# Masked row maxima in attention: the diagonal mask moves from a matrix product into the maximum instruction

## The reference

```
attn = einsum('bhqd,bhkd->bhqk', q, k) / sqrt(hd)
attn = attn + alibi
attn = where(causal, attn, finfo.min)
p    = softmax(attn, axis=-1)
out  = einsum('bhqk,bhkd->bqhd', p, v).reshape(Bb, Tt, C) @ Wo + bo
```

## Time and profile before

| | us |
|---|---|
| median of 3 runs | 1429.78 (1424.3 to 1432.53) |
| span of the profiled execution | 1444.0 |
| main part of the attention stage in it (395 to 960 from the start of the span) | 565 |

### The profile page before, as it was taken

One profiled execution on the slowest core, in us unless ns is written; L12 is line 12 of the kernel. 1 busy time (PEld: TensorE's weight loads), 2 busy tenths in 40 slices (PEclk: granted clock), 3 DMA queues, 4 the chain that ended last, 5 costly groups with the idle time before them and its releaser, 6 DMA issues. The chain is left out here.

```text
span 1444.0 us, 20692 instructions
## 1 busy us (share of the span) xinstructions
PE 1081.1 (75%) x6895; PEld 632.7 (44%) x6896; DVE 790.8 (55%) x2091; ACT 517.8 (36%) x814; POOL 501.2 (35%) x538
## 2 busy tenths in 40 slices
PE   5762149903898999999999989887476877676676
PEld 4651136702244444444454444433244766565443
DVE  4757810044867787878778887761252333333326
ACT  1330013403066556655566545554211221111113
POOL 3110064055016101520154103342444256665633
PEclk9975568955589999999999989987699898999898
DMA  4226013323213111311222121013431432222135
GB/s 117 73 63 109 1 39 106 92 43 91 67 28 97 36 37 47 97 36 36 73 80 80 44 68 52 25 38 143 164 102 34 105 86 77 82 80 63 37 107 185
DMA packets 90021, 106.09 MB, mean 73 GB/s; under 512 B 16882, under 2 KB 69883, under 8 KB 87285
## 3 DMA queue, kind: packets, MB, share of 16 engines
q1 hardware_dynamic: 76862, 79.08, 19.1%
q0 software_dynamic: 13072, 25.90, 6.5%
HBM read 63.29 MB, written 37.95 MB: 70 GB/s over the span
## 5 line engine op out<-in xcount | busy, mean ns | idle before, releaser
L2005 DVE TENSOR_REDUCE maxima<-psum 128x1 f32<-128x512 f32 (+4 forms) x624 | 390.7, 644 | 118.7 <-PE psum L1825 60.7
L1939 ACT ACTIVATE probs<-psum 128x1024 f32<-128x1024 f32 (+3 forms) x384 | 300.6, 809 | 306.8 <-PE psum L1840 237.5
L1820 PE MATMUL psum<-ka,qa 75*128 75x512 bf16 (+3 forms) x768 | 245.4, 352 | 42.6 <-DVE maxima L2005 30.3
L1836 PE MATMUL psum<-qa,ka 78*128 78x512 bf16 (+3 forms) x768 | 211.0, 337 | 4.3 <-ACT probs L1939 4.0
L116 POOL DMA_INDIRECT expert_out<-g_y,g_place x160 | 155.2, 970 | 123.2 <-issue 88.1
L1853 PE MATMUL psum<-probs,v_wide 128*32 128x512 f32 (+3 forms) x1536 | 171.5, 520 | 0.0
L1820 PEld LDWEIGHTS psum<-ka,qa 75*128 75x128 bf16 x768 | 69.6, 101 | 188.7 <-DVE maxima L2005 143.6
L1357 POOL DMA_INDIRECT got<-expert_out,to_row x64 | 66.4, 1038 | 188.0 <-ACT probs L1939 128.4
L2475 DVE TENSOR_TENSOR g_y<-psum,g_gate 128x512 f32<-128x512 f32 x40 | 27.7, 692 | 154.4 <-DMA expert_out<-g_y,g_place 139.3
L1836 PEld LDWEIGHTS psum<-qa,ka 78*128 78x128 bf16 x768 | 75.5, 101 | 79.0 <-ACT probs L1939 28.7
L1840 PE MATMUL psum<-mask_k,ident_b 128*128 128x128 bf16 x512 | 107.1, 228 | 0.0
(11 more groups left out here) (325 smaller groups left out, 1653.2 us busy)
## 6 DMA issues: line engine op xcount, KB each, us to landing
g_rows<-sorted SPq DMA_DIRECT2D x160, 65.0 KB
qa<-q_steps SPq DMA_DIRECT2D x45, 192.0 KB
ka<-k_steps SPq DMA_DIRECT2D x15, 576.0 KB
f_got<-expert_out SPq DMA_DIRECT2D x16, 512.0 KB, 11.1
w<-in_W SPq DMA_DIRECT2D x16, 256.0 KB
w_gu<-in_gu SPq DMA_DIRECT2D x1, 4096.0 KB, 18.6
q_steps<-q_parts SPq DMA_DIRECT2D x12, 256.0 KB
k_steps<-k_parts SPq DMA_DIRECT2D x12, 256.0 KB
```

What stands on the lines that cost most here:

```text
L1820: mm = pe.matmul(bank[:, h * width:(h + 1) * width], qa[b][0:ROWS_MAX, h0 + h, qt * P:(qt + 1) * P], ka[b][0:ROWS_MAX, h0 + h, seg * HALF: ...
L1836: mm = pe.matmul(out, ka[s.buf][0:ROWS_ALL, h, j * P:(j + 1) * P], qa[s.buf][0:ROWS_ALL, h, q0:(c + 1) * HALF], start=True, stop=True, ski ...
L1939: act.activation(probs[k % PRING][:, 2 * pair:2 * pair + 2, 0:w], PS[:, 2 * pair:2 * pair + 2, 0:w], ACT.Exp).then_inc(exps, 1)
L2005: dve.tensor_reduce(maxima[:, seg, h0:h0 + heads, qt], bank[:, 0:heads * width].rearrange("p (h k) -> p h k", h=heads), AX.X, ALU.max).the ...
```

## The change

The 512 mask products of the maxima pass go. `mask_q` (bf16, 128 columns) becomes `mask_wide` (fp32, 512 columns: zeros, then the triangle in the last 128), and VectorE adds its last `width` columns in the same instruction that takes the maximum: `tensor_tensor_reduce`, once for each head instead of once for each unit. It writes the masked scores, which nobody reads, to `masked` (bf16, two buffers), and the maximum to `accum_out`. A wait on `small_read` guards the buffer of two units back. Units below the diagonal keep `tensor_reduce`; the main pass's mask stays a product.

```diff
-        ident_b, mask_q, mask_k = ...
+        ident_b, mask_k = M.sb("ident_b", [P, P], bf16), M.sb("mask_k", [P, P], bf16)
+        mask_wide, masked = M.sb("mask_wide", [P, HALF]), M.sb("masked", [P, 2, HALF], bf16)
...
-                pool.memset(mask_q[:], 0.0).then_inc(preset, 1)
+                pool.memset(mask_wide[:], 0.0).then_inc(preset, 1)
...
-                        if seg * HALF + width == (qt + 1) * P:
-                            for h in range(heads):
-                                mm = pe.matmul(bank[:, (h + 1) * width - P:(h + 1) * width], ident_b[:], mask_q[:],
-                                               start=False, stop=True, skip_group_check=True)
...
+                        if seg * HALF + width == (qt + 1) * P:
+                            if number >= 2:
+                                dve.wait_ge(small_read, number - 1)
+                            for h in range(heads):
+                                last = dve.tensor_tensor_reduce(
+                                    out=masked[:, number % 2, h * width:(h + 1) * width], in0=bank[:, h * width:(h + 1) * width],
+                                    in1=mask_wide[:, HALF - width:HALF], scale=1.0, scalar=LOWEST, op0=ALU.add, op1=ALU.max,
+                                    accum_out=maxima[:, seg, h0 + h, qt:qt + 1])
+                            last.then_inc(small_read, 1)
+                        else:
+                            dve.tensor_reduce(maxima[:, seg, h0:h0 + heads, qt],
+                                              bank[:, 0:heads * width].rearrange("p (h k) -> p h k", h=heads),
+                                              AX.X, ALU.max).then_inc(small_read, 1)
```

More of the change, by code:

```diff
@@ L52 @@
 ROWS_MAX, ROWS_ALL = PROD + 3, PROD + 6
-MASKED = -1.0e30
+MASKED, LOWEST = -1.0e30, -3.0e38
 SCORE_SCALE = float(1 / np.sqrt(np.float32(HD)))
@@ L1642, in stage_attention @@
         recips = [M.sb(f"recip{c}", [P, 4, GH, 2]) for c in range(2)]
-        ident_b, mask_q, mask_k = M.sb("ident_b", [P, P], bf16), M.sb("mask_q", [P, P], bf16), M.sb("mask_k", [P, P], bf16)
+        ident_b, mask_k = M.sb("ident_b", [P, P], bf16), M.sb("mask_k", [P, P], bf16)
+        mask_wide, masked = M.sb("mask_wide", [P, HALF]), M.sb("masked", [P, 2, HALF], bf16)
         max_here = [M.sem(f"max_rows_here{b}") for b in range(BUFS)]
@@ L1728, in _ @@
                                    base=0, pattern=[[-1, P]], channel_multiplier=1).then_inc(masks, 1)
-                pool.affine_select(out=mask_q[:], in_=mask_q[:], compare_op=ALU.is_ge, fill=MASKED,
+                pool.affine_select(out=mask_wide[:, HALF - P:HALF], in_=mask_wide[:, HALF - P:HALF], compare_op=ALU.is_ge, fill=MASKED,
                                    base=0, pattern=[[-1, P]], channel_multiplier=1).then_inc(masks, 1)
@@ L2004, in emit_small @@
                         qt, seg, h0, heads, width = u
-                        dve.tensor_reduce(maxima[:, seg, h0:h0 + heads, qt],
-                                          bank[:, 0:heads * width].rearrange("p (h k) -> p h k", h=heads),
-                                          AX.X, ALU.max).then_inc(small_read, 1)
+                        if seg * HALF + width == (qt + 1) * P:
[11 more added lines that the diff above has]
+                                              AX.X, ALU.max).then_inc(small_read, 1)
                         if u == MAX_UNITS[-2]:
```

## The result

The changed kernel takes 1454.8 us (median of 4 runs, 1444.4 to 1460.4), the kernel before 1427.8. The ratio is 1.018 (95% interval 1.013 to 1.022): slower by 1.8%, where 1419 us was forecast. A second set of runs of the same kernel gave 1.016 (1.007 to 1.025).

A forecast was written before the change was run, and what follows sets the result against it. TensorE was taken to set the pace in most of slots 0 to 9, VectorE in slots 10 and 11. The terms -12 + 2 - 3 + 2 + 0 gave -11 us: 1419 us median, range 1406 to 1465.

The forecast's parts named there:

- What bounds the kernel: Attention stage: TensorE sets the pace in most of slots 0 to 9; slots 10 and 11 wait for VectorE.
- The terms for them, -12 and +2 us: Slots 0 to 9: 12 us gained from removed mask products, 2 us lost to longer many-head units on VectorE.
- The price of the new instruction: VectorE: it takes the plain sum's 281, 418, 555 and 692 ns; the accumulator read costs nothing start to start.
- the half-rate rival: New instruction at half rate, VectorE setting the pace everywhere: 110 us more, 1540; chance 0.06.
- Slots 10 and 11 by hand: Units followed one by one in step 3: about 0.2 us gained, 14 times, 3 us.
- The added wait: VectorE's wait on small_read, 23 times a step: up to 3 us lost, taken as 2.
- the time ahead of step 0: 48 units at half clock ahead of step 0: gains and losses cancel, taken as 0.
- the sum: Whole kernel: -12 + 2 - 3 + 2 + 0 = -11 us, 1419 for the median.
- "a few us": Allowance for the clock in the lower end of the range, beside -16.5 and -3 us.
- a sign to look for afterwards: Sign of being wrong: granted clock of the stretch below 0.96 because TensorE idles more.
- The rival on the other side: VectorE becomes the pace, a head costing 0.15 us above the sum's duration: about +36 us, 1466; chance 0.22.

The follow-up runs named there:

- The wait alone: The kernel before with only the added wait on small_read ahead of the reduction of a diagonal unit; 1431.6 us, ratio 0.999.
- late only: Against the kernel before, the new instruction only in units of slots 0 to 9, early units keep mask product and reduction; 1433.8 us, ratio 1.001.
- No masks: The kernel before without the 512 mask products, nothing in their place, 60 added to the negated maxima; 1444.0 us, ratio 1.010.
- Early only: Against the kernel before, the new instruction only in the eight early units of slots 10 and 11, product and reduction elsewhere; 1457.8 us, ratio 1.019.
- VectorE's part in slots 10 and 11: The kernel before with all mask products kept and the new instruction in the eight early units alone; 1439.1 us, ratio 1.007.
- the kernel with zero products: The changed kernel with the 512 mask products put back on TensorE as products of zeros; 1444.3 us, ratio 1.010 against the kernel before.

## Why the prediction was wrong

**What bounds the kernel**: right. TensorE sets the pace in slots 0 to 9, and at full clock those slots are 0.69 us a step shorter in the mean (0.80 in step 4). The terms for them, -12 and +2 us over 15 steps, are 0.67.

**The price of the new instruction**: right, to 6 ns (549 against 555 is the furthest), and the half-rate rival is out. (That rival took VectorE at 24 us of a step of 35; by the earlier trace rows, 440 of 565, it is 27.) The rule of the Trainium skill (Vector Engine (DVE) Microarchitecture Reference, Points that are easy to get wrong) halves the rate for two SBUF sources that are not bf16, and so by its words spares this form, which ran at full rate. For two SBUF sources the kernel before has a row that goes against it, as far as it goes: a `scalar_tensor_tensor` of two fp32 tiles in SBUF, without an accumulator, takes 688 ns for 512 columns, no more than the sum with one source in PSUM (692). With an accumulator no run here tests it.

```profile
L484 DVE SCALAR_TENSOR_TENSOR qT<-q_exp,qT 128x512 f32<-128x512 f32 x8 | 5.2, 688 | 0.1
```

**Slots 10 and 11 by hand**: wrong, at full clock already. A gain of 0.2 us was worked out for step 3, and it lost 0.29; over the steps at full clock the mean is 0.0 (step 4 gained 0.27), so the 3 us of this term weren't there. The delay of the third unit by the first was right (0.08 worked out, 0.11 found); the gap of 0.26 us ahead of the first new instruction wasn't foreseen. Over all steps these slots grew by 5 us.

**The added wait, and the time ahead of step 0**: taken at 2 and 0 us. The wait alone measured 0.999; the time ahead of step 0 wasn't measured by itself.

**The step that failed is the sum.** It took each slot's gain at full clock and multiplied by 14 and 15. The clock had no term; it stood only as "a few us" at the low end of the range and as a sign to look for afterwards. What the runs show in its place: (a) products taken from TensorE bring the granted clock down, and a kernel with nothing but that edit is 1.0% slower; (b) the 12 products a step missing from slots 10 and 11, where TensorE waits anyway, count by themselves (1.006, clock 0.856), and those of slots 0 to 9 count too (late only 0.858, and 0.841 where all 32 are missing); (c) the half clock that begins in slots 10 and 11 runs on into slots 0 and 1, where TensorE is the pace and each entry costs 3 to 4 us.

At full clock the change gives 0.69 us a step, 10 us in all; measured in the stage is +21, so 31 us went elsewhere. By slots, each with its gain at full clock added back: slots 0 and 1 16 us (15.4 + 14 x 0.07), slots 2 to 9 4.5 (-4.2 + 14 x 0.62), slots 10 and 11 5, steps 14 and 15 5. The last hold a fall of their own (slots 6 to 8 of step 14 at half clock in both profiles); the 4.5 of slots 2 to 9 wasn't followed up.

What the clock costs can be estimated from four kernels. Take a kernel's gain at full clock (per step, from its profile, times 14), add its measured change, and set this against the extra time at half clock in all its executions. No masks: 13 + 15 = 28 us for 72 more at half clock. Early only: 2 + 27 = 29 for 74. Changed kernel: 10 + 25 = 35 for some 90. Late only: 8 + 1 = 9 for 19. By this estimate each microsecond at half clock costs 0.4 to 0.5 us. Such a term was what the sum lacked.

**The rival on the other side** named VectorE as the new pace at 0.15 us more a head, for 1466. The time came near it by another road: no head cost more. VectorE's part in slots 10 and 11 is real, 0.7%, but not by that mechanism's price. It seems to act in two ways: by the wait itself, 0.2 us a step at full clock, some 3 us, and for the rest by the clock, which was 0.857 in its executions against 0.865. Its one profile can't divide them closely (slots 10 and 11 +4 to +7 us over 14 steps, two entries at half clock).

**The time against the range**: 1454.8 lies inside 1406 to 1465, by the width given to the wrong rival.

**What stays open.** Why fewer products bring the clock down, when more of them in the same waits did so too in the kernel before; why the clock comes back within slot 11 in one kernel and not for another 9 us of unbroken products in the other; where most of the 1.0% of the kernel with zero products lies, since its profiled execution was shorter (1435.3) than its median; and how the two parts combine.

## What to carry to other kernels

Before products are taken off TensorE, look at the granted clock by slot. Where it already falls in a wait, taking products from around the wait can keep it down for longer, and the price is paid in the next stretch where TensorE is the bound, at twice the time per column. Make such a change first in the stretches where TensorE is never short of work, try leaving those with waits alone, and compare the granted clock of all executions, not of one profile: here one profile of a kernel could be 18 us off its median. When a stretch is followed, check the result in that stretch, and at full clock first. In this kernel an instruction that serves one head where another served several paid only in units of one head.

## What the runs showed of the hardware

TensorE ran at half clock through 8.97 us in which its records leave no gap (clock 0.52 in that stretch), in products of the same kinds that ran at full clock in the next slots; a second profile has the same (8.83 us at 0.53). Removing 512 products of 128 columns, with nothing in their place, took the granted clock of whole executions from 0.865 to 0.841. VectorE's sum with a running maximum costs what the plain sum costs, 687 ns for 512 columns with one operand in PSUM and a bf16 output, while the read of its accumulator, 81 ns in the records, hides completely behind the next head.
